# Three moves in the order of a fused graph layer's steps: the distance matmuls, a transposition, and a copy on VectorE

## The reference

```python
x = x + relu(norm_adj @ (ln(x) @ W0.T + b0))          # L0_gnn, norm_adj = D^-1/2 adj D^-1/2
x = x + (ln(x) @ Wf.T + bf)                           # L0_ffn
# L1_gnn on xl = ln(x):
h      = relu(bn1(conv1(xl)))                         # 128 -> 128, 1 tap
x_conv = relu(bn2(conv2(h)) + xl)                     # 128 -> 128, 17 taps along the nodes
s      = xl @ w_se.T + b_se                           # 3 numbers per node
A      = exp(-|s_i - s_j|^2) * adj
x_nmp  = A @ relu(xl @ w_msg.T + b_msg)
r, z   = sigmoid(gi_r + gh_r), sigmoid(gi_z + gh_z)   # gi from [x_conv, x_nmp], gh from xl
n      = tanh(gi_n + r * gh_n)
x = x + ((1 - z) * n + z * xl)
for _ in range(30):                                   # L1_ffn on h = ln(x); x = x + h behind it
    h = h + 0.01 * tanh(h); h = h * sigmoid(h)
    h = layernorm(h) * ln_w + ln_b; h = h @ W1.T + b1
```

## Time and profile before

| | us |
|---|---|
| median of three runs | 1403.44 (1402.3 to 1403.54) |
| the profiled execution, as a run | 1402.61 |
| its span, first to last instruction | 1400.6 |
| PE busy | 1330.8 (95%) |
| DVE busy | 1241.4 (89%) |
| ACT busy | 1010.9 (72%) |
| POOL busy | 949.6 (68%) |
| PE waits for DVE's `emb_n` | 10.9, 15 times |
| PE waits for DVE's adjacency copy | 10.3, 13 times |

### The profile page before, as it was taken

The page is one execution under the profiler, slowest core; times in us unless marked ns, Lnnn a source line. Parts: engine busy times, 40 slices in busy tenths (PEclk is TensorE's granted clock), DMA queues, the critical chain, the costliest instruction groups (busy, mean ns, idle before and its releaser), DMA issues.

```text
span 1400.6 us, 28231 instructions
## 1 busy us (share of the span) xinstructions
PE 1330.8 (95%) x8786; PEld 1083.5 (77%) x8786; DVE 1241.4 (89%) x2774; ACT 1010.9 (72%) x1373; POOL 949.6 (68%) x749
## 2 busy tenths in 40 slices
PE   5899999999999999859999999999999999999998
PEld 3677777777777777638888888888888888888887
DVE  6677777777777777689999999999999999999997
ACT  1344444444444444469999999999999999999994
POOL 2244444444444444359999999999999999999995
PEclk9999999999999999979999999999999999999999
DMA  5111111111111100000000000000000000000004
GB/s 177 38 39 38 38 38 37 37 37 38 37 37 37 37 0 1 0 0 1 0 0 0 0 0 0 0 0 0 0 0 0 0 0 0 0 0 0 0 0 121
DMA packets 29790, 27.68 MB, mean 20 GB/s; under 512 B 3269, under 2 KB 21448, under 8 KB 29640
## 3 DMA queue, kind: packets, MB, share of 16 engines
q1 hardware_dynamic: 29768, 27.41, 6.2%
HBM read 23.21 MB, written 4.19 MB: 20 GB/s over the span
## 4 chain that ended last, share of the span: by engine, by line
PE 72%; DVE 13%; issue 6%; ACT 4%; POOL 2%; SPq 1%; DVEq 1%; DMA 0%; POOLq 0%; ACTq 0%
PE psum L751 34%; PE psum L763 15%; PE psum L747 6%; PE psum L553 4%; PE psum L555 4%; PE psum L554 4%; PE psum L575 2%; POOL ln_rs L441 2%; ACT emb_f L855 2%; DVE emb_n L1177 1%; DVE x_less_n L1161 1%; DVE xh L1059 1%; DVE y_all L1059 1%; DVE x_less_n L1164 1%; PE psum L570 1%
## 5 line engine op out<-in xcount | busy, mean ns | idle before, releaser
L751 PE MATMUL psum<-w_t,y_all 128*128 128x128 f32 x3840 | 494.2, 282 | 0.0
L751 PEld LDWEIGHTS psum<-w_t,y_all 128*128 128x128 f32 x3840 | 448.4, 192 | 54.5 <-issue 54.5
L454 POOL TENSOR_TENSOR f_rs<-f_var,half_neg 128x8 f32<-128x8 f32 x240 | 410.2, 1709 | 49.3 <-DVE f_var L1116 31.7
L1091 DVE BATCH_NORM_STATS2 f_stat<-g_ring 128x6 f32<-128x256 f32 x960 | 340.8, 414 | 4.9 <-ACT g_ring L813 4.7
L458 POOL TENSOR_TENSOR h_ring<-g_ring,f_rs 128x640 f32<-128x640 f32 x240 | 303.0, 1262 | 18.8
L1107 DVE SCALAR_TENSOR_TENSOR u_ring<-t_ring,psum 128x1024 f32<-128x1024 f32 x232 | 278.3, 1200 | 0.0
L763 PE MATMUL psum<-ident,h_ring 128*128 128x128 f32 x1920 | 251.2, 274 | 6.4 <-DVE h_ring L1080 6.4
L813 ACT ACTIVATE g_ring<-u_ring 128x1024 f32<-128x1024 f32 x240 | 253.6, 1057 | 1.7 <-DVE u_ring L1107 1.7
L836 ACT ACTIVATE y_all<-psum 128x1024 f32<-128x1024 f32 x240 | 243.6, 1015 | 8.5 <-PE psum L763 8.5
L822 ACT ACTIVATE t_ring<-psum 128x1024 f32<-128x1024 f32 x232 | 238.3, 1027 | 13.8 <-PE psum L751 5.6
L763 PEld LDWEIGHTS psum<-ident,h_ring 128*128 128x128 f32 x1920 | 219.9, 142 | 7.1 <-issue 3.8
(11 more groups left out here) (158 smaller groups left out, 1774.9 us busy)
## 6 DMA issues: line engine op xcount, KB each, us to landing
work<-in_adj_dram SPq DMA_DIRECT2D x16, 1024.0 KB, 5.4
x_tok<-in_x_dram SPq DMA_DIRECT2D x16, 256.0 KB, 5.6
out_dram<-y_all SPq DMA_DIRECT2D x8, 512.0 KB, 3.2
work<-in_L_gnn_conv_w_dram SPq DMA_DIRECT2D x1, 1088.0 KB
work<-in_L_gnn_w_ih_dram SPq DMA_DIRECT2D x1, 384.0 KB
work<-in_L_gnn_w_hh_dram SPq DMA_DIRECT2D x1, 192.0 KB
work<-in_L_gnn_W_dram SPq DMA_DIRECT2D x1, 64.0 KB, 5.0
work<-in_L_ffn_weight_dram SPq DMA_DIRECT2D x1, 64.0 KB, 4.7
```

Source lines behind the costliest of these rows:

```text
L454: pool.tensor_tensor(f_rs[:, j % 4, :], f_var[:, j % 2, :], half_neg[:, 0:GT], ALU.pow).then_inc(f_pow, 1)
L751: m = pe.matmul(y_ps[k % 2][:, h, C * t:C * t + C], y_all[:, GT * k + NT * h + t, :], w1_t[:], start=False, stop=True, skip_group_check=True)
L1091: ins = dve.bn_stats(f_stat[:, j % 2, q, :], both)
```

## The change

```diff
--- before.py
+++ after.py
@@ -649,7 +649,7 @@
-                conv2(4, 7)
+                conv2(4, 8)
                 if later(b):
 
                     pe.wait_ge(s_upd, b)
@@ -660,7 +660,7 @@
                     m.then_inc(s_back, 1)
                 dist(0)
                 dist(1)
-                conv2(7, 15)
+                conv2(8, 15)
                 if l0:
                     if later(b):
                         pe.wait_ge(s_x3, b)
@@ -707,14 +707,14 @@
                     product(bank[TURN_B], w(HH + 2), x_in).then_inc(s_ghn_ps, 1)
-                if l0:
-                    turn(2, c)
-                if l1:
                     x_c, x_n = cut(x_conv, 0, N), cut(x_nmp, 0, N)
                     pe.wait_ge(s_x_conv, 2 * b + 1)
                     pe.wait_ge(s_x_conv_lo, b + 1)
                     product(bank[DIST_A], w(IH), x_c, start=False, stop=False)
                     product(bank[DIST_B], w(IH + 2), x_c, start=False, stop=False)
+                if l0:
+                    turn(2, c)
+                if l1:
                     pe.wait_ge(s_x_nmp, b + 1)
                     pe.wait_ge(s_x_nmp_lo, b + 1)
                     product(bank[DIST_A], w(IH + 1), x_n, start=False).then_inc(s_r_ps, 1)
@@ -1222,16 +1222,16 @@
                 if d is not None:
                     adjt_odd(d, p, 1)
-                if l0:
-                    if b is None:
-                        weights_low(4, 6)
+                if l0 and b is None:
+                    weights_low(4, 6)
                     norm(2, c)
-                    if b is None:
-                        weights_low(6, 7)
+                    weights_low(6, 7)
                 if d is not None:
                     adjt_odd(d, p, 3)
-                    if b is not None:
-                        stats(0, d)
+                if l0 and b is not None:
+                    norm(2, c)
+                if d is not None and b is not None:
+                    stats(0, d)
```

## The result

The changed kernel took 1390.21 us (median of four runs, 1389.84 to 1390.54) against 1403.49 for the kernel before (1402.3 to 1403.82). The ratio is 0.9901, with an interval of 0.9882 to 0.992: 13.3 us less. The forecast was 1388.0 with a range of 1385.5 to 1394.2. The profiled execution took 1390.53 us with a span of 1388.6, which is 12.0 less than the 1400.6 before.

A forecast was written before the change was run, and what follows sets the result against it. PE and what it waits for were taken to set each graph step; 14.0 + 0.1 + 0.6 + 0.7 = 15.4 us less gave 1388.0 against the median of 1403.44, range 1385.5 to 1394.2, 8 in 10.

The forecast's parts named there:

- The adjacency copy, 1.08 a step: Third gate product on PE: its wait for DVE's copy goes entirely, 13 steps x 1.08 = 14.0 us.
- The norm held on its first tile: DVE's norm beside `x_conv_l`: first tile held until POOL ends, three more follow, `x_nmp_l` ends 0.1 us ahead of PE.
- The choice of 0 against 0.37 for the wait: PE ahead of the `x_nmp` products: waits 0 per step, or 0.37 us if the norm kept its whole 2.10; 0 taken.
- The copy is not held by POOL: DVE's adjacency copy beside `x_conv_l`: runs free; if held, 0.46 us lost per step, 1394.0 us in all.
- The turning reaches nothing: Later turning on PE, then ACT's copies, `xc_s_l`, norm and `xs`: still covered at the aggregate, slack 0.5 us.
- The tap in the steps, 0.6: PE's distances one tap later: wait moves to `turn(1)`, distances stay; 7 steps x 0.08 = 0.6 us gained.
- Graph 14, 0.1: Graph 14, no adjacency to turn: PE stands for the norm, which ends with `x_conv_l`; gain 0.1 us.
- Graph 15, 0.7: Graph 15, no `turn(1)`: the moved tap is covered and what follows comes a tap sooner, 0.7 us.
- DVE late by its whole 0.37 a step: Rival at the `x_nmp` products: norm of the whole 2.10 costs 4.8 us, 1392.8; chance 0.22, shared with a held copy.
- The tap did not pay in full: Rival at `turn(1)`: if the norm did not bind it, 14 steps gain 0.70 each, 1378.8 us; chance 0.04.
- The update's chain: Rival, from the turning through `xs` and the gates' sum to `n_act`: late turning slows the step, 1412 us; chance 0.03.
- the order doesn't matter: Rival: PE held by something its waits don't show, nothing moves, 1403 us; chance 0.04.

The follow-up runs named there:

- the experiment with POOL's edges: Changed kernel with POOL's edges(b, p, 0) issued ahead of rstd(1, c) instead of behind it: 1381.54 us, ratio 0.9826 to the kernel before.

## Why the prediction was right

The way, the size and the range held. By its own steps:

- *The adjacency copy, 1.08 a step.* Right in the mechanism, 0.08 too large: copy and turning without the tap gain 13.00 us in 13 steps, 1.00 each, so 13.0 instead of 14.0. The control, graph 0 with 19.16 us, gave 1.10 because its `x_nmp_l` is early there. Where norm 1 is short and DVE therefore ahead, as in the run with POOL's edges first and no tap, the same stretch takes 19.16 us in every step, and the 13 steps take 441.79, 1.11 less each than before.
- *The norm held on its first tile, and `x_nmp_l` at +12.13 from `turn(1)`* (217.77 against 205.64). Measured: +12.13. The norm's end was forecast at 1.67 from its start and is 1.67. The choice of 0 against 0.37 for the wait was right as to the mechanism; 0.06 of the 0.37 came after all. PE starts these products 0.15 behind the end of `x_nmp_l` (214.97 against 214.82), and the work ahead of them would have let it start at +12.19, only 0.06 behind that end. The prediction counted a margin of 0.1 between the two ends as no wait, and left out that start delay. That makes up most of what the 1.08 was too large by.
- *The copy is not held by POOL.* It took 0.69 us beside `x_conv_l`. The Trainium skill (SBUF — State Buffer, section Who interferes with whom) says that a VectorE instruction with one input from SBUF or none, outside the two-port modes, does not contend; the run without the tap and with POOL's edges first agrees, where the copy begins 0.14 us behind POOL and takes 0.69.
- *The turning reaches nothing.* Right: no new wait for `xc_s_l` or `xs`. By itself it is worth 0, behind the copy 0.41 a step.
- *The tap in the steps, 0.6.* Measured 0.40 alone and 0.43 in the changed kernel. The distances stayed where they were, 8.66 us behind the embedding product's end (230.60 against 221.94), as forecast. `turn(1)` starts 0.147 us behind the norm's end in every step, alternately at +14.77 and +14.89 from the embedding product. The wait moved, as the experiment with POOL's edges shows from the other side.
- *Graph 14, 0.1:* nothing; 32.87 us from its embedding product to the next against 32.84. The term had no row of its own and should have been 0: PE now stands there for `x_conv_l`, as long as it stood for the norm before, 1.2 us.
- *Graph 15, 0.7.* Right by itself, 0.75 with the tap alone and 0.73 in the run with `x_nmp_l` moved, the two profiles that show it. In the profile of the changed kernel the half clock took 1.5 us and turned the term into +0.8; a second stretch at half clock in the gates of graph 15 took some 0.6 more.

So of the 15.4 us some 1.3 were mis-sized (1.0 for the copy, 0.3 for the tap and graph 14), which leaves 14.1. The medians give 13.3, and the rest is near what the clock takes or gives in single runs, 0.6 to 1.1 us. In the profiled execution: 13.4 in the steps, less 0.1 at the start, less 1.3 behind graph 15's embedding product, is the 12.0 of the span. Those 1.3 are 0.8 up to the second distances, 0.6 in the gates, 1.0 gained back where the last stage starts, and 0.9 lost again in that stage. The last two nearly cancel, so the last stage kept its length in the sum, as the prediction had it, though not in its parts.

The range was 8.7 us wide, and the kernel without the tap (1392.51) lies in it too. So the time alone bears out the copy and the turning; that the tap's wait moved rests on the profiles.

The rivals: DVE late by its whole 0.37 a step did not come, and 0.06 of it did; the copy was not held. The tap did not pay in full, until POOL's move made it. The update's chain was not reached. That the order doesn't matter is ruled out by the 13.43 us that went in the steps.

## What to carry to other kernels

When a matmul engine waits twice in a loop for the same other engine, look where each wait's chain begins: work pulled ahead of the first wait only pays if the second chain hangs on it, and here it hung on an earlier product, so the wait moved. A control inside the same trace (the first graph, without the wait) gives the size of a wait better than the idle time in the row, which was 0.8 where the cost was 1.0. And an instruction that takes twice its usual time beside a neighbour's work may be cured by the neighbour's order: here that was worth two thirds of the whole change (8.4 us) with the tap moved, and 4.2 us in the steps of the kernel before.

## What the runs showed of the hardware

- Four `tensor_scalar` instructions on fp32 in SBUF of 128x128 take 1.11 us, but one of them took 0.90 and 1.32 in the rows shown where it began beside POOL's 512-column operation, and ended 0.08 us behind it. A copy out of PSUM beside the same operation keeps its 0.69, whether it begins 0.13 us before it or 0.14 behind it.
- PE's granted clock can fall to half behind a gap of 3.0 to 3.7 us with only four transposes in it. In five profiles it stayed there for about 3.5 us of dense matmuls, which costs 1.5 to 1.6 us; in three (the copy alone, and POOL's edges first in the two kernels without the tap) for about twice as long, which costs 2.5 to 2.8. Two kernels with the same gap differed in it, while the same kernel showed it at the same place in both of its profiles.
- The last stage of the changed kernel was 12.85 us ahead of the kernel before near 640 us, and only 12.0 near 770. One iteration of this stage, eight groups, takes PE 25.41 us at first and 25.77 later, in every kernel alike, and the changed kernel came to the slower pace sooner. In 500 us of the slower part DVE is busy throughout. What sets the pace wasn't tried.
